# Column means of squares in a transformer layer: 1-column matmuls replaced by four column tiles and a block transpose

## The reference, cut to what matters

```python
def rmsnorm(x, w):
    return x * jax.lax.rsqrt(jnp.mean(x * x, axis=-1, keepdims=True) + EPS) * w
tokens = tokens + merge_heads(masked_attn(q, k, v, valid)) @ out_w.T + out_b
query = rmsnorm(tokens, sq_norm_w)
...
tokens = tokens + gate * update
h = rmsnorm(tokens, ffn_norm_w)
```

## Time and profile before

| | before |
|---|---|
| median of 3 runs | 577.9 us (568.83, 577.9 and 583.28) |
| the profiled execution | 576.22 us, of which the span from the first to the last instruction is 574.4 us |
| mean granted TensorE clock | 0.887 of full speed |
| busy in the span | PE 81%, PEld 55%, DVE 57%, ACT 51%, POOL 40% |

### The profile page before, as it was taken

One profiled execution on the slowest core, in us unless ns is written; L12 is line 12 of the kernel. 1 busy time (PEld: TensorE's weight loads), 2 busy tenths in 40 slices (PEclk: granted clock), 3 DMA queues, 4 the chain that ended last, 5 costly groups with the idle time before them and its releaser, 6 DMA issues.

```text
span 574.4 us, 12792 instructions
## 1 busy us (share of the span) xinstructions
PE 466.5 (81%) x4994; PEld 317.0 (55%) x4994; DVE 326.3 (57%) x612; ACT 293.8 (51%) x651; POOL 232.1 (40%) x228
## 2 busy tenths in 40 slices
PE   4434598787877898898999889898999799887785
PEld 3213386664765685665667557565676475443331
DVE  2106579854856776686658655676457666323122
ACT  3042167655555567466746663766446446542422
POOL 4154262431613154364716463344414423443633
PEclk9856579978878889799999999999689989997889
DMA  3544545615444244425233624151401400000000
GB/s 101 136 142 122 161 123 140 170 40 165 108 139 138 79 144 117 140 68 174 79 115 89 167 72 141 56 166 37 139 21 41 129 4 21 2 19 0 19 18 19
DMA packets 64077, 54.03 MB, mean 94 GB/s; under 512 B 4044, under 2 KB 61842, under 8 KB 64018
## 3 DMA queue, kind: packets, MB, share of 16 engines
q1 hardware_dynamic: 63908, 53.20, 32.2%
q10 hardware_dynamic: 110, 0.02, 0.0%
HBM read 8.49 MB, written 2.11 MB: 18 GB/s over the span
## 4 chain that ended last, share of the span: by engine, by line
PE 39%; SPq 18%; DMA 13%; POOL 9%; ACT 9%; issue 8%; DVE 4%; POOLq 0%; ACTq 0%; DVEq 0%
SPq L567 14%; PE ps_o L330 7%; PE ps_g L256 5%; PE ps_g L382 5%; PE ps_a L293 5%; PE ps_b L313 5%; DMA q_st<-part_q 4%; PE ps_g L369 3%; DMA q_st<-top_t 3%; DMA k_st<-part_k 2%; ACT probs L780 2%; DMA swap_q<-part_q 2%; POOL hid L668 2%; PE ps_g L280 1%; DMA s_in<-in_fside_BxSxS 1%
## 5 line engine op out<-in xcount | busy, mean ns | idle before, releaser
L936 DVE TENSOR_REDUCE top<-ps_a 128x4 f32<-128x512 f32 x256 | 169.8, 681 | 129.3 <-PE ps_a L293 128.3
L780 ACT ACTIVATE probs<-ps_b 128x512 f32<-128x512 f32 x256 | 149.9, 596 | 161.4 <-PE ps_b L313 160.8
L293 PE MATMUL ps_a<-k_st,q_st 73*128 73x128 bf16 x1024 | 108.9, 234 | 35.9 <-DMA k_st<-part_k 10.3
L293 PEld LDWEIGHTS ps_a<-k_st,q_st 73*128 73x128 bf16 x1024 | 74.0, 105 | 89.0 <-issue 60.3
L313 PE MATMUL ps_b<-q_st,k_st 75*128 75x128 bf16 x1024 | 104.1, 227 | 13.8 <-ACT probs L780 7.3
L313 PEld LDWEIGHTS ps_b<-q_st,k_st 75*128 75x128 bf16 x1024 | 71.7, 102 | 21.5 <-issue 9.5
L330 PE MATMUL ps_o<-probs,v_pad 128*32 128x128 f32 x2048 | 78.6, 301 | 0.0
L330 PEld LDWEIGHTS ps_o<-probs,v_pad 128*32 128x32 f32 x2048 | 58.6, 120 | 25.7 <-issue 14.9
L665 POOL TENSOR_SCALAR unit_th<-unit_th 128x512 f32<-128x512 f32 x32 | 20.1, 629 | 106.3 <-ACT unit_th L794 106.3
L640 POOL TENSOR_TENSOR full_q<-full_q,swap_q 128x512 f32<-128x512 f32 x8 | 10.2, 1270 | 93.7 <-DMA swap_q<-part_q 93.7
L256 PE MATMUL ps_g<-norm,w_t 128*128 128x512 f32 x80 | 45.8, 657 | 2.8 <-ACT hid L796 1.6
(11 more groups left out here) (125 smaller groups left out, 662.2 us busy)
## 6 DMA issues: line engine op xcount, KB each, us to landing
q_st<-part_q SPq DMA_DIRECT2D x144, 128.0 KB
k_st<-part_k SPq DMA_DIRECT2D x144, 128.0 KB
x_in<-in_x SPq DMA_DIRECT2D x16, 256.0 KB, 4.3
s_in<-in_fside_BxSxS SPq DMA_DIRECT2D x8, 256.0 KB, 6.3
swap_q<-part_q SPq DMA_DIRECT2D x16, 128.0 KB, 2.5
upd<-part_k SPq DMA_DIRECT2D x16, 128.0 KB, 2.3
out<-t SPq DMA_DIRECT2D x8, 256.0 KB, 3.1
probs<-in_L_cond_gu_w SPq DMA_DIRECT2D x2, 256.0 KB, 3.7
```

The costliest lines, as they stand in the source:

```text
L293: mm = pe.matmul(ps_a[q % 2][:, j * S:(j + 1) * S], st[0][i][0:R_MAX, h, b * S:(b + 1) * S], st[1][i][0:R_MAX, h, b * S:(b + 1) * S], star ...
L780: act.activation(probs[:, n % 2, q * T:(q + 1) * T], ps_b[q % 2][:, :], ACT.Exp, scale=SCALE).then_inc(exp_done, 1)
L936: dve.tensor_reduce(top[:, n // 2 % 2, n % 2, QH * q:QH * (q + 1)], ps_a[q % 2][:, :].rearrange("p (h k) -> p h k", h=QH), AX.X, ALU.max). ...
```

## The change

The matrix of 1/128 becomes 128x32 and is now the stationary operand. For each quarter u of the tokens of every batch (32 tokens), the squares of the four batches move past it (128 columns, four runs of 32), and the result goes to partitions 32u to 32u + 31 of the bank: 32 equal rows, with the token within the quarter and the batch along the free dimension. VectorE then turns the 128x128 result in blocks of 32x32 from PSUM into the tile `quotient`, waits for that, and adds EPS to the first column of each block, which gives the same 128x4 tile as before. The bank counts as empty once the transpose is done. A new semaphore mean_set tells GpSimd's `root` and the next user of `quotient` that the means are there; since ss2 and ss3 of different groups alternate, `mean_rank` gives each its place in the order.

```diff
-        mean_w = sb("mean_w", [D, 1])
+        mean_w = sb("mean_w", [D, 32])
...
+        mean_order = sorted([(c_prep(g), "ss2", g) for g in range(G)] + [(after(g) + 21, "ss3", g) for g in range(G)])
+
+        def mean_rank(key):
+            return [one[1:] for one in mean_order].index(key) + 1
...
             def column_means(key, t, squares):
+
                 to, done = take(key, t, 2)
-                for b in range(NG):
-                    mm = pe.matmul(to[:, b:b + 1], squares[:, b * S:(b + 1) * S], mean_w[:, :], start=True, stop=True)
+                for u in range(4):
+                    mm = pe.matmul(to[32 * u:32 * u + 32, 0:S], mean_w[:, :],
+                                   squares.rearrange("d (b u t) -> d u b t", b=NG, u=4)[:, u], start=True, stop=True)
                 mm.then_inc(done, 1)
...
                 ms, r, done, key = ((ms2, r2, root2_set, ("ss2", g)), (ms3, r3, root3_set, ("ss3", g)))[which]
-                taken(pool, key)
+                pool.wait_ge(mean_set, mean_rank(key))
                 pool.tensor_tensor(r[:, :], ms[:, :], minus_half[:, :], ALU.pow).then_inc(done, 1)
...
+            means_taken, pairs_divided = [0], [0]
+
...
                 dve.wait_ge(inverse_set, m + 1)
                 wait(dve, att_set, m)
+                wait(dve, mean_set, means_taken[0])
+                pairs_divided[0] = m + 1
                 dve.tensor_tensor(
...
             def mean_of(key, ms):
+
                 src = full_in(dve, key)
-                dve.tensor_scalar(ms[:, :], src[:, 0:NG], EPS, None, ALU.add).then_inc(taken_sem(key), 1)
+                wait(dve, att_set, pairs_divided[0])
+                wait(dve, mean_set, means_taken[0])
+                dve.transpose(quotient[:, 0:S], src[:, 0:S]).then_inc(taken_sem(key), 1)
+                taken(dve, key)
+                means_taken[0] += 1
+                assert mean_rank(key) == means_taken[0]
+                dve.tensor_scalar(ms[:, :], quotient[:, 0:S].rearrange("p (b c) -> p b c", c=32)[:, :, 0], EPS, None,
+                                  ALU.add).then_inc(mean_set, 1)
```

More of the change, by code:

```diff
@@ L196, in build @@
         top_in = [sem("top_in0"), sem("top_in1")]
+        mean_set = sem("mean_set")
         inverse_set, quotient_set, att_set = sem("inverse_set"), sem("quotient_set"), sem("att_set")
@@ L453, in _ @@
                         taken(pe, ("out", g))
-                        column_means(("ss2", g), t, norm2)
+                        column_means(("ss2", g), t, norm2[:, :])
                     if t == c_prep(g):
@@ L473, in _ @@
                         pe.wait_ge(sq3_set, g + 1)
-                        column_means(("ss3", g), t, gate_th)
+                        column_means(("ss3", g), t, gate_th[:, :])
                     if t == after(g) + 24:
```

## The result

| | before | changed |
|---|---|---|
| median | 578.4 us (6 runs, 568.8 to 583.3) | 562.5 us (6 runs, 555.2 to 573.6) |
| ratio | | 0.971, 95% interval 0.965 to 0.978 |
| second set, on another chip | 574.7 us (11 runs) | 568.7 us (6 runs, 560.4 to 570.8), 0.984 (0.976 to 0.991) |
| profiled execution, its span | 574.4 us | 556.8 us |
| mean granted clock in it | 0.887 | 0.914 |

The change is faster, by 16 us in the first set and by 6 us in the second; the means of all executions differ by 14.2 and 7.9. I had forecast 2.0. The forecast missed 562.5 by 13 us, and the time lies under the range. One program's executions spread over 15 us or more, and the ratios leave the slow ones out, so I give medians and means of all beside them.

The account below looks back on a forecast made before the run. No engine alone bounds the kernel; the chain is 39% TensorE, 31% DMA and its issue. Savings of 0.54 + 0.86 + 0.73 - 0.1 = 2.0 us take the median from 577.9 to 575.9 us; range 568.5 to 583.

Parts of the forecast that it names:

- What VectorE pays: VectorE's added transpose and addition in each use of column_means: bank free 0.16 us later, means there 0.35 us later.
- All of it counts: Rival: TensorE's saving in all 16 uses of column_means counts, 6.9 us won, 571.0 us; chance 0.18.
- the nine events: Nine of the 16 uses of column_means, where the chain does not pass; their saving was counted as nothing.
- The event on TensorE: One use of column_means on TensorE: 0.45 us instead of 0.88, saving 0.43.
- my 0.23 for entering and leaving the tiled form: TensorE's switch of tiling mode in each use of column_means: 0.10 us to enter plus 0.13 to leave.
- the stretching that I had as a rival: Stronger form of the VectorE-or-root rival (chance 0.14): VectorE's SBUF addition stretched by 0.87 us beside GpSimd, 597 us.
- Group 2's event: The ss2 use of column_means at 210 us: root ends later than its slack allows, about 0.1 us lost.
- Group 5's: The ss2 use of column_means at 352 us: starts 0.35 us earlier, takes 0.35 longer, so gains 0.
- The event at half clock: The ss3 use of column_means at 544 us, granted clock 0.50: 0.73 us saved of 1.50.
- The waits for the bank at 261 us: value_unit waits for VectorE to empty the means' bank, at 261 and 423 us: 0.43 less 0.16, 0.27 us saved each.
- the two full events: The ss3 uses of column_means at 464 and 493 us: full saving of 0.43 us each, 0.86 together.
- the seven: The seven uses of column_means judged able to affect the chain, at 210, 261, 352, 423, 464, 493, 544 us: 2.0 us saved.

Follow-up runs that it names:

- the pads: Kernel before plus an unused 96-byte tile: behind mean_w 570.4 us (again 568.2), ahead of the stacks 567.4, behind the stacks 578.4, declared last 577.8.
- f3: Kernel before with the four matmuls of column_means issued twice in the nine events the prediction counted at nothing: median 579.3 us, 3.2 over before.
- The doubled runs: Kernel before with the four matmuls of column_means issued twice: in all 16 events 587.8 us, in nine 579.3, in the other seven 586.8.
- f4: Kernel before with the four matmuls of column_means issued twice in the seven events where the predicted chain passes: median 586.8 us, 10.7 over before.
- e8: Kernel before with the four matmuls of column_means issued twice in all 16 events: median 587.8 us, 11.5 over before.

## Why the prediction was wrong, point by point

- **The step that failed** stands at the end of "What VectorE pays". The prediction said that "the wider memset and GpSimd's other semaphore cost nothing", and looked at the line that widens `mean_w` only for its memset. Its effect on the addresses is not in the sum, and it is the largest term: -8.3 us, shown by the pads, which change no work. No rival had it either. Between the pooled means the whole change is 12.0 us (577.1 to 565.1): about 8 for the place of the stacks and 4.3 for the events. What the first set shows beyond that (15.9 by the medians) lies in the spread of six executions; the second set has 6.0. "All of it counts", at 571.0, came nearest by the number. It names the events for what is mainly the place, though f3 shows that it was right in part: the nine events are not free.
- **The event on TensorE**: 0.36 us instead of 0.45, between the bound of 0.25 and the forecast. By the same working, my 0.23 for entering and leaving the tiled form would be 0.14 (0.36 less two steps of 0.11). 0.52 saved instead of 0.43.
- **VectorE**: 0.309 and 0.187 us instead of 0.31 and 0.15, so the means are there 0.50 us after the start of the transpose, as forecast (207.90 to 208.40 at group 2). One of the 16 additions took 0.449, beside an instruction of GpSimd (L673, 0.62 us), the stretching that I had as a rival; in the median it is 0.170. It decided nothing: GpSimd waited for this tile in 13 of the 16 cases (the earlier trace rows had 11).
- **Event by event.** Group 2's event was to lose 0.1: from the event to the factors it lost 0.15, though through a late maximum more than through the root. I had written that TensorE needs that maximum "only for the next but one ps_a"; here this was already too soon. Group 5's was to gain 0 and gained 0.44; GpSimd's root ends 0.41 us after the start of the matmul that reads it (342.37 + 1.01 against 342.97), so its recorded end cannot be used to work out a slack. The root's own rows:

```profile
342.37 1.01 POOL L643 TENSOR_TENSOR f<-f 128x4 f32<-128x4 f32 x1 [2.50 <-DVE f L995]
```

- The event at half clock, 0.73 forecast, in the changed kernel:

```profile
529.01 0.66 PE L358 MATMUL ps_g<-gate_th,mean_w 128*32 128x128 f32 x8
529.84 2.08 PE L262 MATMUL ps_g<-norm,w_t 128*128 128x512 f32 x2 [0.18 <-DVE hid L1022]
```

  0.83 to the next start instead of 1.57, 0.74 saved. The waits for the bank at 261 us became longer, as forecast, by 0.15 (0.39 in the earlier trace rows):

```profile
253.97 0.43 PE L358 MATMUL ps_g<-norm,mean_w 128*32 128x128 f32 x8 [0.42 <-ACT norm L815]
...
256.39 1.13 PE L377 MATMUL ps_g<-norm,w_t 128*128 128x512 f32 x2 [0.54 <-DVE quotient L991]
```

  From the event to the matmul that waits for its bank it is 2.42 us instead of 2.78, so 0.36 saved where I had 0.27. With the rows above and 0.52 in the two full events, the seven sum to 0.36 x 2 + 0.52 x 2 + 0.74 + 0.44 - 0.15 = 2.8 us instead of 2.0.
- **The sum of the events**: 2.0 forecast, 4.3 +- 2.0 measured. The forecast is within the error, and the mechanism holds as far as the timelines show it; the size in the whole time is not settled. The doubled runs show why the forecast may be too small: an event off the chain is worth 0.4 of its time, not 0. That a chain names one of several nearly equal paths would explain it, but was not tried. With 0.52 saved in each of the nine, this adds 1.9 us to the 2.8 above; 4.7 is an estimate from these figures.
- **The range** took the spread of one program's executions for its ends, and no term for what a changed declaration does to the placement.

## What to carry to other kernels

Read a diff for its declarations as well as for its instructions. A tile that grows moves every tile behind it, and the pads here show that this alone was worth about twice what the work was (8.3 us, and 4.3 with an error of 2.0). Before crediting a change of work with some per cent, compare it with the old work at the new addresses, and repeat the comparison: five executions of one program gave a ratio of 0.984 against itself. The chain of an execution ranks the places at which time counts, and doubling the work there measures what it is worth, if the granted clock of the doubled place is read too.

## What was not expected of the hardware

- Moving the SBUF tiles that DMAs fill by 64 to 96 bytes changed the kernel's time by 8.3 +- 0.9 us of 577. It follows neither the remainder by 64 bytes (64 further, same remainder: -9.2; 32 further, other remainder: -4.2) nor the tiles behind the stacks (+1.8). The sum of the times of the same 37392 packets of 1024 bytes goes from about 2000 to about 1950 us. Why the old place is bad is open.
- Four column tiles of 128x32 with 128 float32 columns each take 0.36 us from start to next start between matmuls of the full array, 0.83 at a granted clock of 0.50 with 0.18 of waiting in it.
- Eight more MATMULs of one column made an event take 3.27 us at a granted clock of 0.50, where it had taken 0.88 at 1.00 (f4 and e8, against the kernel before). The 6.9 us planned in seven events became 8.6 in the trace and 10.7 in the time.
